# Second layer of a two-layer graph attention kernel: a small clear on GpSimd ahead of every gather from the ninth on

## The reference, cut to what matters

```python
h = relu(layernorm(x))                    # x after the first layer
q, k, v = h @ W_q.T + b_q, h @ W_k.T + b_k, h @ W_v.T + b_v
z = (q @ k.T) / sqrt(512)
z = z * adj
z = where(z == 0, -10000, z)              # only neighbours count
x = x + relu(softmax(z, axis=1) @ v)
```

## Time and profile before

| | us |
|---|---|
| median of 3 runs | 454.66 |
| the profiled execution, its own time | 451.98 |
| its span in the trace | 450.1 |
| POOL busy | 255.9 |
| DVE busy | 368.4 |
| PE busy | 393.3 |

### The profile page before, as it was taken

The page is one execution under the profiler, slowest core; times in us unless marked ns, Lnnn a source line. Parts: engine busy times, 40 slices in busy tenths (PEclk is TensorE's granted clock), DMA queues, the critical chain, the costliest instruction groups (busy, mean ns, idle before and its releaser), DMA issues.

```text
span 450.1 us, 6244 instructions
## 1 busy us (share of the span) xinstructions
PE 393.3 (87%) x2058; PEld 281.5 (63%) x2070; DVE 368.4 (82%) x731; ACT 245.7 (55%) x511; POOL 255.9 (57%) x268
## 2 busy tenths in 40 slices
PE   7999999998799998999977997978998999968860
PEld 4888887786588886886554755645656855434430
DVE  3999999986899999998799999689854568989900
ACT  4379777783999999872442443343433346142220
POOL 2335151321868866876786535883524777788640
PEclk9599999999899999999996999989999999989995
DMA  8988999710000023435755432763212676679941
GB/s 322 395 347 316 380 313 350 272 50 25 4 6 6 7 29 91 103 112 151 232 155 148 151 95 87 208 208 112 95 47 96 193 207 200 200 171 130 127 61 19
DMA packets 26996, 70.02 MB, mean 156 GB/s; under 512 B 7892, under 2 KB 8148, under 8 KB 24788
## 3 DMA queue, kind: packets, MB, share of 16 engines
q0 software_dynamic: 13056, 38.45, 32.4%
q1 hardware_dynamic: 13904, 31.16, 19.0%
q10 hardware_dynamic: 4, 0.00, 0.0%
HBM read 52.47 MB, written 17.13 MB: 155 GB/s over the span
## 4 chain that ended last, share of the span: by engine, by line
POOL 28%; DVE 16%; issue 15%; PE 11%; DMA 2%; ACT 1%; DVEq 0%; POOLq 0%
PE psum L1349 7%; POOL s_shared L1271 7%; POOL s_shared L1300 5%; POOL out_dram L1284 4%; POOL s_shared L1252 3%; POOL s_rs L1282 3%; DVE s_shared L814 3%; DVE s_shared L812 3%; DVE s_shared L1044 3%; POOL s_x L1290 2%; POOL s_early L1300 2%; PE psum L1450 2%; DVE s_x L828 2%; DVE s_shared L821 1%; DVE h_t L1044 1%
## 5 line engine op out<-in xcount | busy, mean ns | idle before, releaser
L1101 ACT ACTIVATE s_shared<-psum,seq_all 128x320 bf16<-128x320 f32 x192 | 81.9, 571 | 6.0 <-PE psum L1349 4.3
L1349 PE MATMUL psum<-s_shared 128*128 128x198 bf16 x768 | 75.1, 254 | 9.6 <-POOL s_shared L1252 9.6
L1349 PEld LDWEIGHTS psum<-s_shared 128*128 128x128 bf16 x768 | 67.9, 98 | 17.4 <-POOL s_shared L1252 9.9
L563 PE MATMUL psum<-w_seq,hT 128*128 128x272 f32 x256 | 63.3, 402 | 0.4 <-ACT w_seq L424 0.4
L1371 PE MATMUL psum<-w_out,hT 128*128 128x512 f32 x128 | 61.4, 625 | 0.4
L563 PEld LDWEIGHTS psum<-w_seq,hT 128*128 128x128 f32 x256 | 49.0, 195 | 10.2 <-ACT w_seq L424 0.5
L1393 PE MATMUL psum<-w_qk,s_early 128*128 128x257 f32 x240 | 54.5, 379 | 0.0
L1393 PEld LDWEIGHTS psum<-w_qk,s_early 128*128 128x128 f32 x240 | 44.3, 189 | 6.0
L1271 POOL DMA_INDIRECT s_shared<-seq_dram,tab x30 | 37.4, 1246 | 11.3 <-issue 8.9
L1371 PEld LDWEIGHTS psum<-w_out,hT 128*128 128x128 f32 x128 | 26.2, 205 | 26.3 <-issue 25.4
L282 POOL TENSOR_TENSOR rstd<-veps,power 128x1 f32<-128x1 f32 x16 | 8.9, 558 | 54.9 <-DVE veps L468 54.9
(11 more groups left out here) (267 smaller groups left out, 742.1 us busy)
## 6 DMA issues: line engine op xcount, KB each, us to landing
adj_ring<-in_adj_dram SPq DMA_DIRECT2D x16, 1024.0 KB, 7.8
seq_dram<-seq_all POOLq DMA_DIRECT2D x16, 264.0 KB, 4.0
x_ring<-in_x_dram SPq DMA_DIRECT2D x16, 256.0 KB, 8.2
h_dram<-h_t SPq DMA_DIRECT2D x16, 256.0 KB, 2.3
w_seq<-in_L_gnn_W_seq_dram SPq DMA_DIRECT2D x1, 1024.0 KB, 5.5
w_q<-in_L_gnn_W_q_dram SPq DMA_DIRECT2D x1, 1024.0 KB, 13.5
w_k<-in_L_gnn_W_k_dram SPq DMA_DIRECT2D x1, 1024.0 KB, 15.7
w_v<-in_L_gnn_W_v_dram SPq DMA_DIRECT2D x1, 1024.0 KB, 8.6
```

The source lines that it names most:

```text
L563: last = pe.matmul(bank[2 + 2 * (t % 2) + i][:, 0:SX // 2], hT[:, t % 2, c * P:(c + 1) * P], w_seq[:, c, i * (SX // 2):(i + 1) * (SX // 2) ...
L1101: last = act.activation(ind[i][:, j, PAD:], bank[4 + i][:, 0:LN], ACT.Sign, bias=seq_all[:, j, D + n:D + n + 1])
L1349: last = pe.matmul(acc(i)[:, k, 0:3 * W2], ind[i][:, j, k * P:(k + 1) * P], rhs.rearrange("p t w -> p (t w)"), start=(j == 0 and k != 1), ...
```

## The change

From gather k = 8 on, a `memset` of 128 x 320 float32 in the idle tile `sc` is put in front of the gather; it raises the semaphore `paused` by one. From k = 9 on, a wait for `paused >= k - 8` stands in front of that memset. The value is reached when the memset ahead of the gather before is done.

```diff
+        BREAK_FROM = 8
+        paused = sem("paused")
+        idle = sc[:, 0:20, :]
         ROWS_EARLY = FLAT_ROWS + C + LONE + 1
...
                 def gather1(t):
                     for s in range(SLOTS[t]):
                         k = ROW1[t] + s
+                        if k >= BREAK_FROM:
+                            if k > BREAK_FROM:
+                                pool.wait_ge(paused, k - BREAK_FROM)
+                            pool.memset(idle, 0.0).then_inc(paused, 1)
                         if k == ROWS_EARLY:
```

## The result

Median of four runs each on one chip: before 454.60 us (453.88 to 454.87), with the change 464.81 us (464.00 to 465.22), ratio 1.0225 [1.0206, 1.0244]. The prediction said 463.9 us, range 459.5 to 469.7.

A forecast was written before the change was run, and what follows sets the result against it. The prediction took GpSimd's gathers to set the end, with 0.84 us of VectorE slack; clears 8.6, waits 0, landing 0 and TensorE 0.6 sum to +9.2 us on 454.66, so 463.9 us, range 459.5 to 469.7.

The forecast's parts named there:

- What bounds the kernel: Second layer's gathers on GpSimd set the end; VectorE came free only 0.84 us before the last rows landed.
- The clears, 8.6 us: 32 added memsets between gathers on GpSimd, each with a 0.37 us record, add 0.27 us each.
- the nearer reading: An elementwise instruction between two indirect DMAs adds its record less 0.11 us: 0.26 us a clear.
- the spacing of starts: Consecutive memsets' start-to-start times on GpSimd give 0.31 us a clear, 9.9 us for 32.
- The waits, nothing: 31 memsets' waits for `paused` on GpSimd are always over when their turn comes, so cost nothing.
- Starts 1.53 us apart and the last gather issued at 406.6: Expected on GpSimd's timeline after the change: gathers start 1.53 us apart rather than 1.26, the last issued at 406.6 us.
- Landing, 0 +/- 1: Last gather's time from issue to landing, 4.38 us before, may move by -0.9 to +1.0 us; taken as 0.
- TensorE after the hole, 0.6 us: After about 7 us idle, TensorE's lower clock makes tile 13's products 1.8 us longer; 0.6 us reach the end.
- The sum, +9.2 us: Whole kernel: 8.6 + 0 + 0 + 0.6 us, added to the runs' median, gives 463.9 us.
- Hides in the issue gap: Rival: clears vanish in the 0.30 us between gathers, 2.2 us in all or 0; chance 0.08.
- Costs more than its record: Rival: each clear on GpSimd adds 0.39 to 0.63 us, giving 467.8 to 475.3 us; chance 0.13.
- Faster: Rival: spaced-out gathers get cheaper, by 2.2 us together, capped by VectorE at 0.84 us: 453.8 us; chance 0.03.

The follow-up runs named there:

- e7: Kernel before, no clears, second-layer gathers fetch 128 instead of 512 columns (a quarter of the bytes, output wrong): 452.96 us, 0.9985 to before.
- e2: Changed kernel with clears of 128x1 instead of 128x320, on chip 9: 484.84 us, 0.9995 to the kernel before there.
- e3: Changed kernel with clears of 128x576 instead of 128x320, on chip 9: 468.89 us, 0.9653 to the kernel before there.
- e4: Changed kernel in which each gather also waits for the clear directly ahead of it, on chip 9: 467.51 us, 0.9624 to the kernel before there.
- one pause: Kernel before plus four chained 128x576 clears ahead of gather 10 only, on chip 13: 457.03 us, 1.0077 to before.
- e6: Changed kernel with a clear and its wait ahead of every fourth gather only, eight instead of 32, on chip 13: 457.69 us, 1.0090 to before.
- e5: Kernel before, unaltered, traced again on chip 13: 455.15 us in one run.
- e12: Changed kernel with 30 and 34 idle TensorE matmuls put into its two holes, on chip 3: 465.93 us, 1.0272 to before.
- e10: Changed kernel with 24 and 22 idle TensorE matmuls put into its two holes, on chip 3: 465.84 us, 1.0269 to before.
- e1: Changed kernel, unaltered, run again on chip 9: 463.38 us, 0.9538 to the kernel before, which took 485.57 us there.
- e11: Changed kernel with VectorE's aggregate1 of tiles 13 and 15 moved ahead of tile 5's dots, on chip 3: 460.04 us, 1.0138 to before.

## Why the prediction was right, and where it wasn't

- **What bounds the kernel: right.** All that delayed the last gather went to the end, VectorE stood waiting at tile 5's first dot, for 5.52 us (5.7 said), and e7 confirms that GpSimd sets the pace.
- **The clears, 8.6 us: right in kind, 1.1 too much.** 0.235 us each rather than 0.27, 7.5 us; the nearer reading (0.26, from an instruction between two DMAs) beat the spacing of starts (0.31). The record is 0.38 us (0.37 said), and 0.16 us behind it rather than 0.17. e2 and e3 fix the form: some 0.14 us of record is swallowed by the issue gap, and beyond that each addition counts in full.
- **The waits, nothing: right.** No trace of the change has an idle time ahead of a clear, and e4 shows what real waits would have cost, 4.0 us.
- **Starts 1.53 us apart and the last gather issued at 406.6: half right.** Ordinary pairs stand 1.50 apart, but the last gather was issued at 409.83. The forecast had no term for longer gather records, +3.2 us. Every kernel with clears of 320 or 576 columns has an excess of 3.2 to 5.1 us, every one without (before, quarter rows, 128x1) 1.1 to 1.4 and one pause 1.56.
- **Longer gather records: a term that the prediction put at nothing.** It comes with the clears, and the traces show with what it goes: VectorE's instructions. Of the 448 gathers from k = 8 in all fourteen traces 166 have records of 1.00 us or more. Each of them began while one of VectorE's 128x512 instructions (a dot or a multiply-add) was running, and ended 0.82 to 0.84 us after that instruction did; the 186 that met none of these stayed within 0.98 us. With the change:

```profile
384.91 0.68 DVE L1006 CUSTOM_DVE_ANT_0 w_seq<-seq_all,s_shared 128x512 f32<-128x512 f32 x1
385.15 1.28 POOL L1307 DMA_INDIRECT s_lone<-h_dram,s_near_rank  x1 [0.17 <-issue]
```

  A gather so pays for what is left of VectorE's instruction at its start, less 0.12 us. (Fourteen others began within 0.07 us of that instruction's own start; these weren't held.) Clears change where in it the gathers start: of the 32, ten met one with more than 0.12 us left in before, 0.25 us on average, and 16 in the change, 0.39 us on average. A few clears can shift the gathers as well as many, which fits e6. No experiment took VectorE's instructions away.
- **Landing, 0 +/- 1: right.** 4.15 us; before had 4.40 and, in e5, 5.48.
- **TensorE after the hole, 0.6 us: right in mechanism, too small.** 1.6 us from the two traces, 1.4 by e12. The slow stretch cost tile 13 3.0 us where 1.8 was said: 3.0 less the 1.2 of slack is 1.8. The rows at 401.60 from which the 1.8 came were clocked at 0.79 over their window, these at 0.57. The step that failed is taking the one slow stretch in the trace for the price of any. It isn't the length of the idle time that makes the difference: behind 3.69 or 3.70 us of it the eight matmuls took 4.98 us in before, 5.29 in e5 and 5.96 in e10, behind 5.93 us 5.93. The idle time was forecast at 7 us and came as 5.93, since tile 11's aggregation, and with it the products ahead of the hole, ended later than forecast too.
- **The sum, +9.2 us.** Medians show +10.2 here, +11.2 on chip 3; the two profiled executions differ by 13.1. The profiled before was 2.6 us under its median, and the profiled after 0.2 over its own, so that these two overstate the difference. The median came out 0.9 us over the forecast, and that close it came by luck in part: of the 3.2 and 1.0 us that were missing, the oversized clear term made good 1.1, and the start and the last landing some 2, which against e5 came 0.7 and 1.3 us sooner with the change.
- **The rivals.** (The excess of the records before sums to 1.16 us, not to 1.3 as the prediction has it, which decides nothing.) "Hides in the issue gap" holds for a 128x1 clear (e2) and not for this one. "Costs more than its record" holds for no clear. "Faster" named shorter gather records; they became longer.
- **What no rival had**: that the sign depends on the chip. On chip 9 the clears save 22 us. By e2's trace that is time in which TensorE's signals are held back, which is a reading of the trace and not shown by an experiment. e2 tells that neither the waits nor a 128x1 clear, which doesn't stretch the gap, helps, and e1, e3 and e4 that gaps longer throughout by 0.235 us or more do; single pauses of 0.91 and 1.48 us late in e2 didn't. Why that chip and no other, where in it the signals are held, and what spacing is enough, is open; the trace of before on the first chip, from which the forecast was made, has nothing of it.

## What to carry to other kernels

Work put between two indirect DMAs on GpSimd costs its record less about 0.14 us when GpSimd sets the pace, and a wait that is over beforehand costs nothing. It also shifts where each gather falls against VectorE's instructions, which here cost nearly half as much again (3.2 us beside 7.5); so price the instruction, then ask who falls idle downstream and what that idleness costs a second time on TensorE. Where an engine must wait, move ready work into the wait (e11) rather than filling it with dummy work (e12). And time a kernel that leans on long unbroken runs of indirect DMAs on more than one chip before you settle a change of 2%.

## What the runs showed of the hardware

- **Signals late beside a stream of gathers, as far as the traces tell.** On one of the chips seen, gathers 1.26 us apart went with an evacuation 35 us late and some 30 us of standstill (e2); 1.50 us apart, with one 4.4 us late and no standstill (e1). The same kernel took 485.57 us there and 452.97 to 454.60 on the others.
- **GpSimd and VectorE hold each other up.** A gather is held by a running 128x512 instruction of VectorE (166 records, above). The other way round, in the changed kernel's timeline of DVE two small instructions, which take 0.17 us in before, end with GpSimd's instruction: one with a clear, at 370.74, one with a gather, at 371.86:

```profile
370.40 0.37 DVE L1022 TENSOR_SCALAR hT<-hT 128x24 f32<-128x24 f32 x1
...
371.23 0.60 DVE L1025 TENSOR_SCALAR hT<-hT 128x3 f32<-128x3 f32 x1
```

```profile
370.35 0.39 POOL L1302 MEMSET s_sc<- 128x320 f32 x1
370.90 0.96 POOL L1307 DMA_INDIRECT s_shared<-h_dram,s_near_rank  x1 [0.16 <-issue]
```

  The Trainium skill (SBUF — State Buffer, Who interferes with whom) has one port pair that VectorE and GpSimd share under an exclusive lock; the ends that meet agree with it. The small instructions are off the chain that ended last; the gathers are on it.
- **TensorE's clock.** It stayed full after holes of up to 2.45 us (e10) and fell after 3.69, 3.70, 5.93 and 7.55 us; the eight matmuls then took 4.98, 5.96, 5.93 and 5.48 us instead of 3.60, so that the longer hole wasn't the dearer one.
- **The last branch of a longer TensorE program** cost 3.4 us (e10, e12), more than the 1.4 us that the added matmuls were to win.
